# Expert results added to the output in DRAM by accumulating indirect stores, instead of stored, gathered and summed

## The reference

```python
x = x + L1_gnn(xn, ...) + L1_mix(xn, ...)          # called x3 in the kernel
z = layernorm(x)
rh = relu(z @ router_w1 + router_b1)
logits = softmax(rh @ router_w2 + router_b2)       # 6 experts
top_w, top_i = top_k(logits, 2)
share = softmax(top_w)
h1 = relu(z @ expert_w1[e] + expert_b1[e])
h2 = relu(h1 @ expert_w2[e] + expert_b2[e])
y[e] = h2 @ expert_w3[e] + expert_b3[e]
x = x + sum over the two chosen e of share[e] * y[e]
```

## Time and profile before

| | us |
|---|---|
| median of 3 runs | 6301.56 (6300.48 to 6309.79) |
| the profiled execution | 6297.91 |
| its span | 6295.7 |
| routing loop, from 5594 to 5820 | 226 |
| from the last round to the first tile, 5820 to 5847 | 27 |
| expert loop, 5847 to 6154 | 307 |
| gather tail, 6154 to 6296 | 142 |

### The profile page before, as it was taken

One profiled execution on the slowest core, in us unless ns is written; L12 is line 12 of the kernel. 1 busy time (PEld: TensorE's weight loads), 2 busy tenths in 40 slices (PEclk: granted clock), 3 DMA queues, 4 the chain that ended last, 5 costly groups with the idle time before them and its releaser, 6 DMA issues.

```text
span 6295.7 us, 87281 instructions
## 1 busy us (share of the span) xinstructions
PE 5271.7 (84%) x24977; PEld 4430.6 (70%) x24977; DVE 3384.1 (54%) x9879; ACT 1311.4 (21%) x2962; POOL 3878.9 (62%) x4349
## 2 busy tenths in 40 slices
PE   0165766499999999989999899999999999987894
PEld 0154655267777777777888787778887788866782
DVE  9866666445555555455446544555455554547223
ACT  0011111011111111133224322331112311111340
POOL 5767777765655555688888883316763167636006
PEclk9976888699999999999999999999999999998995
DMA  1022122233333333611001101223332144453324
GB/s 43 24 79 81 55 63 58 83 104 98 100 99 98 101 98 98 69 46 42 17 16 39 39 17 27 82 65 100 104 100 80 62 114 114 109 95 96 97 89 133
DMA packets 319773, 477.58 MB, mean 76 GB/s; under 512 B 99008, under 2 KB 240054, under 8 KB 319470
## 3 DMA queue, kind: packets, MB, share of 16 engines
q0 software_dynamic: 153136, 262.81, 17.0%
q1 hardware_dynamic: 166334, 211.17, 10.9%
HBM read 371.27 MB, written 102.33 MB: 75 GB/s over the span
## 4 chain that ended last, share of the span: by engine, by line
PE 68%; DMA 10%; POOL 8%; DVE 8%; issue 4%; ACT 1%; DVEq 0%; SPq 0%; ACTq 0%; POOLq 0%
PE bank L2384 18%; PE bank L2395 14%; POOL scratch_sorted L1013 7%; DMA scratch_sorted<-sb_FREE 6%; PE bank L2430 6%; PE bank L2445 6%; PE bank L2612 5%; PE bank L2594 5%; PE bank L2881 3%; PE bank L2737 3%; PE bank L2375 2%; DMA sb_rows<-scratch_xn,sb_row_of 2%; PE bank L2923 1%; DVE sb_STATE L1498 1%; DMA sb_HT<-scratch_ys,sb_srec 1%
## 5 line engine op out<-in xcount | busy, mean ns | idle before, releaser
L1020 POOL DMA_INDIRECT sb_rows<-scratch_xn,sb_row_of x1760 | 1718.4, 976 | 1430.9 <-PE bank L2430 605.5
L1013 POOL DMA_INDIRECT scratch_sorted<-sb_FREE x1564 | 1608.2, 1028 | 486.8 <-issue 330.6
L2395 PE MATMUL bank<-sb_work_FT,sb_W 128*128 128x250 f32 x4400 | 1008.9, 381 | 20.4 <-ACT sb_work_FT L1100 16.0
L1100 ACT ACTIVATE sb_HT<-bank,sb_cols 128x250 f32<-128x250 f32 x1333 | 553.7, 467 | 1979.1 <-PE bank L2594 1060.9
L2395 PEld LDWEIGHTS bank<-sb_work_FT,sb_W 128*128 128x128 f32 x4400 | 846.5, 193 | 135.7 <-ACT sb_work_FT L1100 23.5
L2384 PE MATMUL bank<-sb_W,sb_HT 128*125 128x256 f32 x4000 | 893.4, 380 | 0.7 <-ACT sb_HT L1100 0.7
L2384 PEld LDWEIGHTS bank<-sb_W,sb_HT 128*125 128x125 f32 x4000 | 752.5, 188 | 115.0 <-ACT sb_HT L1100 1.1
L2445 PE MATMUL bank<-sb_rows,sb_work_TM 128*125 128x257 f32 x1760 | 471.4, 392 | 72.7 <-DMA sb_rows<-scratch_xn,sb_row_of 72.2
L1822 DVE TENSOR_TENSOR sb_STATE<-sb_STATE,bank 125x257 f32 x440 | 185.5, 422 | 623.0 <-PE bank L2445 594.1
L1767 DVE TENSOR_TENSOR sb_FREE<-sb_FREE,bank 125x257 f32 x440 | 185.8, 422 | 620.1 <-PE bank L2430 584.8
L2430 PE MATMUL bank<-sb_rows,sb_work_TM 128*125 128x257 f32 x1760 | 440.1, 389 | 34.4 <-DMA sb_rows<-scratch_xn,sb_row_of 25.2
(11 more groups left out here) (392 smaller groups left out, 7008.5 us busy)
## 6 DMA issues: line engine op xcount, KB each, us to landing
sb_rows<-scratch_xn,sb_row_of POOLq DMA_INDIRECT x1760, 2.8
scratch_sorted<-sb_FREE POOLq DMA_INDIRECT x1564, 2.4
scratch_qT<-sb_work_QF SPq DMA_DIRECT2D x100, 250.0 KB
sb_work_QF<-scratch_qT SPq DMA_DIRECT2D x100, 250.0 KB
sb_work_XC<-in_x SPq DMA_DIRECT2D x50, 250.0 KB
sb_work_ZT<-scratch_xn SPq DMA_DIRECT2D x50, 250.0 KB
sb_W<-in_L_mix_W SPq DMA_DIRECT2D x9, 1024.0 KB
sb_work_XC<-scratch_zs SPq DMA_DIRECT2D x28, 256.0 KB, 2.6
```

What stands on the lines that cost most here:

```text
L1013: nc.gpsimd.indirect_dma_start(out=sorted_d[e], out_offset=bass.IndirectOffsetOnAxis(ap=pos[e][0:n, c:c + 1], axis=0), in_=rec[e][0:n, 2 * ...
L1020: nc.gpsimd.indirect_dma_start(out=rows[:, t % RING, 0:D], out_offset=None, in_=table, in_offset=bass.IndirectOffsetOnAxis(ap=row_of[:, t: ...
L1100: return nc.scalar.activation(dst, source, func, **k)
L2395: ins = nc.tensor.matmul(dst[:, b, :], w[:, k0 + k, 128 * (b0 + b):128 * (b0 + b) + 128], source[:, k, :], start=(n == 0), stop=(n == 2 * ...
```

## The change

The routing loop also puts five numbers behind each z row: the token's number, its two experts, its two shares; rows of `zs` are 261 floats instead of 256. One small DVE copy a round writes the token numbers (`row`, ahead of `z`); experts and shares are now written there by the operations that made them before. SP stores x3 to the output in the routing loop. The experts' third biases are loaded for all 128 partitions. The padding rows are now written by SP, 256 rows at a place read into a register, six DMAs; their token number is 65536, outside of the output. Each expert's capacity grows by a tile, so that these always fit.

In the expert loop DVE works out, of the loaded tile, the share of each row in this expert (`shares`, `share`) and the row's number as an integer (`at`); rings of eight. DVE's copy of c's result becomes a sum with the third bias. ACT then multiplies each row by its share, in place. POOL adds the rows to the output: two indirect DMAs of 128 rows with the operation add, per tile; each tile waits until the previous tile's have landed. A row whose number is over 6249 is left out. The `ys` tensor, the gather tail, its matrix products and its place and share tables on DVE are gone.

The core of the diff:

```diff
-C1_DVE = (... "pair", "gdif") + named(1, "z")
+C1_DVE = (... "pair", "gdif") + named(1, "row", "z")
-CAP = TILE * ((N + 2 * TILE - 1) // TILE)
+CAP = TILE * ((N + 2 * TILE - 1) // TILE + 1)
-X_ACT = named(2, "turn") + named(1, "a") + named(0, "b")
-X_DVE = named(2, "w0", "bias") + named(1, "w1") + named(-1, "y")
+X_ACT = named(2, "turn") + named(1, "a") + named(0, "b") + named(-1, "y")
+X_DVE = named(2, "w0", "bias", "shares", "share", "at") + named(1, "w1") + named(-1, "y")
+SRING = 8
+ROW, OWNER, SHARE, DW = D, D + 1, D + 3, D + 5
...
 # SP, routing loop
+                if j == NP - 4:
+                    sp.dma_start(bexp1, ...to_broadcast([128, NEXP1, D])).then_inc(weights_loaded["exp_rest"], 16)
+                if j:
+                    store_x3(j - 1)
 # SP, padding
+            sp.wait_ge(pads_ready, 2)
+            for e in range(NEXP1):
+                at = sp.value_load(pad_rows[0:1, e:e + 1], min_val=0, max_val=NEXP1 * CAP - TILE)
+                sp.dma_start(zs_d[bass.ds(at, TILE), :].rearrange("(p u) n -> p (u n)", u=2), zero_rows)\
+                    .then_inc(pads_stored, 16)
 # SP, expert loop
-                    sp.dma_start(by_tile(ys_d)[:, t, :], YB[t % XRING]...).then_inc(y_stored[t % XRING], 16)
+                wait(sp, x_pe.done("turn", t))
+                wait(sp, x_dve.done("at", t))
+                load_tile(t + XRING)
 # POOL, in the place of padding scatters and gathers
+            pool.wait_ge(out_stored, 16 * NC)
+            for t in range(NX):
+                q = t % XRING
+                wait(pool, x_dve.done("at", t))
+                wait(pool, x_act.done("y", t))
+                if t:
+                    pool.wait_ge(result_added, 32 * t)
+                hold(pool)
+                for u in range(2):
                     nc.gpsimd.indirect_dma_start(
+                        out=out, out_offset=bass.IndirectOffsetOnAxis(ap=OUT_AT[:, t % SRING, u:u + 1], axis=0),
+                        in_=YB[q][:, u, :], in_offset=None, bounds_check=N - 1, oob_is_err=False,
+                        compute_op=ALU.add).then_inc(result_added, 16)
 # ACT
+                    wait(act, x_dve.done("y", t))
+                    for u in range(2):
+                        ins = move(YB[t % XRING][:, u, :], YB[t % XRING][:, u, :], scale=SHAREOF[:, t % SRING, u:u + 1])
 # DVE
+                    nc.vector.tensor_copy(ZR[(j + 1) % ZN][:, 0:r, ROW:ROW + 1], ROWID[:, ch:ch + r]...)
...
+                    dve.wait_ge(tile_loaded[q], 16 * (t // XRING + 1))
+                    if t >= SRING:
+                        dve.wait_ge(result_added, 32 * (t - SRING + 1))
+                    nc.vector.scalar_tensor_tensor(SHARES[:, t % SRING], XB[q][:, :, OWNER:OWNER + 2], exp_all[:, t:t + 1],
+                                                   XB[q][:, :, SHARE:SHARE + 2], ALU.is_equal, ALU.mult)
+                    nc.vector.tensor_reduce(SHAREOF[:, t % SRING], SHARES[:, t % SRING], AX.X, ALU.add)
+                    nc.vector.tensor_copy(OUT_AT[:, t % SRING], XB[q][:, :, ROW])
...
-                        wait(dve, (y_stored[t % XRING], 16 * (t // XRING)))
-                    nc.vector.tensor_copy(YB[t % XRING], PSUMS[t % 2]...)
+                        dve.wait_ge(result_added, 32 * (t - XRING + 1))
+                    nc.vector.tensor_tensor(YB[t % XRING], PSUMS[t % 2]..., bexp1[:, bass.ds(of_tile[t], 1), :]..., ALU.add)
```

More of the change, by code:

```diff
@@ L114 @@
 C1_DVE = (named(1, "x3", "stats", "mean") + named(0, "logit", "lmax", "lsub") + named(1, *RSQRT)
-          + named(0, "lsum", "lrec", "p", "max", "arg", "argf", "one", "pair", "gdif") + named(1, "z")
+          + named(0, "lsum", "lrec", "p", "max", "arg", "argf", "one", "pair", "gdif") + named(1, "row", "z")
           + named(0, "gsum", "g1", "g2", "at", "prod", "pos", "index", "add", "acc"))
 TILE = 256
-CAP = TILE * ((N + 2 * TILE - 1) // TILE)
+CAP = TILE * ((N + 2 * TILE - 1) // TILE + 1)
 CAP_TILES = CAP // TILE
@@ L482, in carve @@
             return spare[0:of, taken[0] - n:taken[0]]
[L484 to L486 removed]
+        POS = carve(2 * NT, T).bitcast(U32).rearrange("p (t k) -> p t k", k=2)
+        POSF = carve(2 * NT, T).rearrange("p (t k) -> p t k", k=2)
+        ROWID = carve(NT, T)
         ONE, PROD = (carve(64, T).rearrange("p (t k e) -> p t k e", t=4, k=2) for _ in range(2))
@@ L489, in build @@
         ACC, CAPS, ADD = (carve(8, T) for _ in range(3))
-        ZR = [QT, [tok(W0[:, 1024:2048].rearrange("p (s n) -> p s n", s=2), s) for s in range(2)],
-              [tok(HT[:, :, 4:8, :].rearrange("p s b n -> p s (b n)")[:, :, 0:2 * D], s) for s in range(2)]]
+        wide_ht = HT[:, :, :, :].rearrange("p s b n -> p (s b n)")
+        wide_rows = rows[:, :, :].rearrange("p q n -> p (q n)")
+        ZR = [x[0:T, at:at + 4 * DW].rearrange("p (t n) -> p t n", t=4)
+              for x, at in ((wide_ht, CH), (wide_ht, 9 * CH), (wide_rows, 0))]
         ZN = len(ZR)
@@ L499, in build @@
         LM4, GD4, GA4, RV4, RY4, RT4 = (four(x) for x in (LM, GD, GA, RV, RY, RT))
-        pad_from, pad_at = (carve(2 * NEXP1).rearrange("p (h e) -> p h e", h=2) for _ in range(2))
-        pad_rows = carve(2 * NEXP1).bitcast(U32).rearrange("p (h e) -> p h e", h=2)
+        pad_at = carve(NEXP1, 1)
+        pad_rows = carve(NEXP1, 1).bitcast(I32)
         tilesT, beganT, endedT = (carve(1, 8) for _ in range(3))
@@ L505, in build @@
         exp_of, in_of = (carve(NX, 1).bitcast(I32) for _ in range(2))
+        exp_all = carve(NX)
+        SHARES = carve(4 * SRING).rearrange("p (q u k) -> p q u k", q=SRING, u=2)
+        SHAREOF = carve(2 * SRING).rearrange("p (q u) -> p q u", q=SRING)
+        OUT_AT = carve(2 * SRING).bitcast(U32).rearrange("p (q u) -> p q u", q=SRING)
         BIAS = carve(4 * XRING).rearrange("p (q m u b) -> p q m u b", q=XRING, m=2, u=1)
         WX = [[part(W0, 1024 * m + 512 * s, 2, D) for s in range(2)] for m in range(2)]
-        zero_rows = rows[:, 0, 0:D]
+        zero_rows = wide_rows[:, 4 * DW:6 * DW]
         def halves(name):
             return [work[name][:, s, :].rearrange("p (k n) -> p k n", k=2) for s in range(2)]
-        XB, YB = halves("XC") + halves("ZT"), halves("KT") + halves("TM")
+        XB = [wide_ht[:, 2 * DW * q:2 * DW * (q + 1)].rearrange("p (u n) -> p u n", u=2) for q in range(XRING)]
+        YB = halves("KT") + halves("TM")
         XT, H1, H2 = halves("FT"), halves("QF"), halves("QT")
[L516 to L524, removed]
         def xs(n, w=1):
@@ L912, in load_xn1, with store_x3 @@
                 sp.dma_start(ZT[s], tiles(xn1_d)[:, n:n + 2, :]).then_inc(xn1_read[s], 16)
+            def store_x3(j):
+                wait(sp, c1_dve.done("x3", j))
+                for s in slots_of(j):
+                    n = 4 * j + 2 * s
+                    sp.dma_start(tiles(out)[:, n:n + 2, :], XM[:, n:n + 2, :]).then_inc(out_stored, 16)
             for s in range(2):
                 load_xn1(0, s)
-            load("exp_up", (bexp1, a["L1_ffn_expert_b3"]), *[expert(0, e) for e in range(NEXP1)])
-            sp.wait_ge(routing_cleared, 8)
+            load("exp_up", *[expert(0, e) for e in range(NEXP1)])
+            sp.wait_ge(routing_cleared, 6)
             for j in range(NP):
@@ L944, in _ @@
                 load_tile(t)
[L945 to L958, removed]
+            for t in range(NX - XRING):
+                wait(sp, x_pe.done("turn", t))
+                wait(sp, x_dve.done("at", t))
+                load_tile(t + XRING)
             sp.wait_ge(out_stored, 16 * NC)
+            sp.wait_ge(result_added, 32 * NX)
         @block.gpsimd
@@ L1072, in _ @@
                             out=zs_d, out_offset=bass.IndirectOffsetOnAxis(ap=POS[:, 4 * j + n, k:k + 1], axis=0),
[L1073 to L1077, removed]
-                    nc.gpsimd.indirect_dma_start(
[L1079 to L1094, removed]
+                            in_=ZR[j % ZN][:, n, :], in_offset=None).then_inc(z_scattered[j % ZN], 16)
+            pool.wait_ge(out_stored, 16 * NC)
[7 more added lines that the diff above has]
+                for u in range(2):
+                    nc.gpsimd.indirect_dma_start(
+                        out=out, out_offset=bass.IndirectOffsetOnAxis(ap=OUT_AT[:, t % SRING, u:u + 1], axis=0),
+                        in_=YB[q][:, u, :], in_offset=None, bounds_check=N - 1, oob_is_err=False,
+                        compute_op=ALU.add).then_inc(result_added, 16)
         @block.scalar
@@ L1299, in _ @@
                     relu_tile(b, "b", H2, PC, 1)
[L1301 to L1306, removed]
+                t = b - 1
+                if t >= 0:
+                    wait(act, x_dve.done("y", t))
+                    for u in range(2):
+                        ins = move(YB[t % XRING][:, u, :], YB[t % XRING][:, u, :], scale=SHAREOF[:, t % SRING, u:u + 1])
+                    ins.then_inc(*x_act.add("y", t))
         @block.vector
@@ L2272, in _ @@
             dve.wait_ge(route_sums, 3)
```

(3 more changed lines are left out.)

132 lines of the change are left out of this document (39 added, 93 removed).

## The result

The changed kernel takes 6239.93 us (median of 4 runs, 6231.55 to 6245.84) beside 6302.27 for the kernel before: a ratio of 0.9896, 95% interval 0.9884 to 0.9908. It is some 1% faster; 6194.5 was forecast, in a range of 6150 to 6340.

The account below looks back on a forecast made before the run. PE alone bounded the expert loop (5.62 us a tile), a chain through DMAs the gather tail. First rows at 5851.4 plus 54 turns of 6.2 gave 6186.2, span 6188.6, median 6194.5 us; range 6150 to 6340.

Parts of the forecast that it names:

- The likeliest case: Expert loop: the additions' serial chain, not PE, sets the pace at 5.7 to 8.1 us a tile, 6167 to 6297; 45%.
- the turn P: Expert loop: one tile's turn of the serial additions, wake 0.77, issue 0.95, gap 0.30 and landing 4.2: 6.2 us.
- the rival's text: Rival that serial additions cost more than the tail did; it said an addition reads twice for each write; slower: 25%.
- the term that decides: Expert loop: the accumulating stores' serial chain, one turn per tile, 2.02 us plus the landing, taken as 4.2.
- The rival that PE stays the bound: Expert loop: PE keeps setting the pace at 5.62 us a tile, with L up to 3.6; time 6156; chance 30%.
- L: Expert loop: time from issue of a tile's second addition to its landing; taken as 4.2 us, bounds 2.4 to 7.5.
- The rival on the other side: Expert loop: serial additions cost more than the tail did, from a turn of 8.18 us, L 6.15; slower: 25%.
- The routing loop: Thirteen rounds, each with one more small DVE copy of 0.2 us: 0.5 us taken, range 0 to 2.6.
- the row of the round: Routing loop: profile of one round, where 0.4 us of cover before PE's transposes makes the extra copy cost nothing.
- Padding: Ahead of the expert loop: six SyncE stores replace twelve POOL scatters; ready 13.2 us earlier, 12.5 taken, bounds 9 and 14.
- The bound of 9: Padding ahead of the expert loop: least gain, 9 us, if the last store lands after 6.7, the longest gather.
- the signs that I named: PE's first turn near 5834; POOL's pace 6.2; DVE idle before its new sum; PE's loop share 0.9; landings giving L.

Follow-up runs that it names:

- the kernel with flags: Changed kernel, but a tile waits for the tile two before, and for the one before only where experts change or neither has one: 6168.3 us, ratio 0.9795.
- kernels with two tiles in flight: Changed kernel with additions waiting for the tile two before: 6167.02 us; the version for any routing, with added flag-dependent waits for the previous tile: 6168.3 us.

## Why the prediction was right, and where its size was off

The likeliest case was the one that came: the additions' serial chain as the bound, PE's share at 0.9 (276.11 of 307), DVE idle ahead of its new sum until an addition landed. The time lies 45.4 us above the forecast. From first issue to last landing I had 54 x 6.2 less the first wake, 334.0 us; it was 6231.60 + 3.8 - 5860.63 = 374.8, or 40.8 more. The first issue came 8.4 later than mine (5860.63 to 5852.2), the span ends 4.6 after the last landing instead of 2.4, and the median of the runs lies 0.07 below the profiled span (6239.93 to 6240.0) where I had put it 5.85 above: 40.8 + 8.4 + 2.2 - 5.9 = 45.5.

*The term that was mis-sized is the turn P*, 6.2 for 6.96, by its three parts. Issue: I took a gather's 0.95, and an addition takes 1.55 (+0.60); I gave it no bounds, and the rival's text already said that an addition reads twice. Landing: 4.2, built from the gather's shortest landing and the scatter's; the second addition of a tile, which is the one that the turn waits for, lands after 4.1 in the mean of the 41 that stand in the chain (-0.1). Wake with the hold: 0.77, for 0.90 after most landings and 0.94 in the mean of the trace's turns (+0.2). That makes 0.7 of the 0.76; the rest is rounding. So the landing, which I called the term that decides, was right within 3%, and the chain got longer by what I had read as safe. That the landing came out so near is in part luck: a gather's read and a scatter's write were put end to end without a row for their sum, and the bounds went from 2.4 to 7.5.

*The rival that PE stays the bound* needed L up to 3.6 with an issue of 0.95. With the issue at 1.55 it needed L under about 2.9, which the stores without add reach (and there PE is the bound) and the additions do not. By the Trainium skill's figure (page "DMA: Bandwidth & Descriptors", "Anatomy of one DMA — SWDGE (gpsimd) path") the landing of 128 KB would be an estimated 2.3; the measured 4.1 decides against it for additions, while the store's 2.41 is close to it.

The Trainium skill's other rule (same page, "Rules for kernel authors": wait for the earlier DMA's semaphore) holds for accesses of the same bytes. The changed kernel keeps it between all neighbours; the kernel with flags keeps it where neighbours can meet, and no run here tried what happens without it.

*The rival on the other side* needed P = 8.18; single steps reach 8.3, the mean does not.

*The routing loop.* From its first to its last router sum it takes 191.1 us (5626.8 to 5817.9) where it took 191.3 (5621.1 to 5812.4): the extra copy is covered, as the row of the round had it, and 0.5 was too much. But the loop began 5.7 us later, by code that is the same; in the other kernels the same point lies anywhere from 5620.3 to 5626.9, and this loop alone took 195 in two of them. Such shifts between executions are in the 8.4 above, 5.7 of it; most of the rest is the padding, 9.7 for the 12.5 taken.

*Padding.* 13.2 worked out, 12.5 taken; the way from the cast to the first tile load got 9.7 shorter (24.7 to 15.0). I had SyncE's spacing from the first tile loads (1.19; measured 1.6), and a landing of 2.0 to 2.6 (measured 5.06): five times 0.4, and 2.5. The bound of 9, with a landing of 6.7, held. Of the signs that I named, PE's first turn near 5834 did not come: it starts at 5843.26, later by the 5.7 of the routing loop's start and by what the padding gained less than worked out (9.7 for 13.2).

*What the wait costs in all.* The chain's turn as the bound costs 369 us for 53 steps where PE needs 298: 71 us of the 142 that went with the tail. The kernels with two tiles in flight show them: 6167 and 6168 for 6240.

## What to carry to other kernels

When a change puts a DMA's round trip into a loop, price each part of the turn apart (wake, issue, gap, landing) and bound each, not only the one that seems unknown: at 1.3 us over the engine's pace, 0.6 of issue mattered as much as anything. Then ask whether the order is needed between all neighbours or between a few: here only tiles of different experts can share a row, and a wait that depends on a flag gave back what the serial one cost. An experiment that keeps the waits and takes the operation away (stores for additions) tells what the operation costs in one run.

## What the runs showed of the hardware

An indirect accumulating DMA of 128 rows of 1 KB takes POOL 1.55 us to issue, beside 0.97 for the same DMA as a store; its landing is 3.9 us, beside 2.8 to 2.9, at the median of all 108 (of the second of a tile in the last step, 3.82 beside 2.41). The queue of POOL's DMAs has three times the packets for it (both from 5840 to 6240: first the kernel with stores in place of additions, then the one with two tiles in flight):

```profile
q0 software_dynamic: 5184, 13.33, 9.1%
```

```profile
q0 software_dynamic: 15552, 13.34, 29.7%
```

15552 packets for 108 additions are 144 each, 48 for a store, at the same bytes. The check of row numbers against a bound cost nothing measurable in the issue (1.55 us with and without). An accumulating DMA of 6.4 MB from DRAM to DRAM took 36.2 us. SyncE's register loads took 0.27 us ahead of the first tile load and up to 1.19 us among the padding stores; what makes the difference was not separated.
